# Fourth attention: score product split into three fp32r products with rounded and low parts

## The reference

```python
h = group_norm(x, gn_w, gn_b)
q = nin(h, Wq, bq).reshape(B, C, H * W)        # C = 128, H * W = 1024
k = nin(h, Wk, bk).reshape(B, C, H * W)
v = nin(h, Wv, bv).reshape(B, C, H * W)
w = jnp.einsum('bcn,bcm->bnm', q, k) * C ** (-0.5)
w = jax.nn.softmax(w, axis=-1)
h_out = jnp.einsum('bnm,bcm->bcn', w, v).reshape(B, C, H, W)
h_out = nin(h_out, Wp, bp)
out = (x + h_out) / math.sqrt(2.0)
```

## Time and profile before

| what | value |
| --- | --- |
| three runs | 537.21, 538.37, 539.49 us |
| median | 538.37 us |
| profiled execution, first to last instruction (span) | 533.3 us |
| profiled execution, whole time | not given |
| PE busy in the span | 474.2 us (89%) |
| POOL busy in the span | 277.2 us (52%) |
| granted PE clock, mean | 0.974 |

### The profile page before, as it was taken

How to read it: one execution, slowest core, us unless ns; L and a number is a source line. 1 busy time by engine, 2 the same in 40 slices (tenths; PEclk the granted TensorE clock), 3 DMA queues, 4 the chain that set the end, 5 groups by cost and what they waited for, 6 DMA issues and landing times.

```text
span 533.3 us, 7633 instructions
## 1 busy us (share of the span) xinstructions
PE 474.2 (89%) x2772; PEld 318.4 (60%) x2772; DVE 320.2 (60%) x567; ACT 288.1 (54%) x514; POOL 277.2 (52%) x292
## 2 busy tenths in 40 slices
PE   7997888698768799899988999998989899998997
PEld 3443534336234368567776847775955668693776
DVE  5767775664727667775586665478477446534322
ACT  5464645664746565256566246575635466623653
POOL 0000477777777777777777777777777500000000
PEclk9699999998989889999999999999999999998999
DMA  6000211122131111113112111112111100100001
GB/s 233 0 1 1 75 50 54 51 77 73 52 98 54 50 55 50 55 50 96 55 54 90 55 50 55 49 56 93 52 54 51 44 1 1 40 1 1 1 1 39
DMA packets 12708, 26.94 MB, mean 51 GB/s; under 512 B 4992, under 2 KB 5888, under 8 KB 12672
## 3 DMA queue, kind: packets, MB, share of 16 engines
q0 software_dynamic: 9216, 18.89, 11.9%
q1 hardware_dynamic: 3168, 7.05, 3.7%
q10 hardware_dynamic: 288, 0.52, 0.3%
HBM read 21.99 MB, written 4.46 MB: 50 GB/s over the span
## 4 chain that ended last, share of the span: by engine, by line
POOL 52%; PE 23%; issue 17%; DVE 4%; ACT 3%; DMA 1%; DVEq 1%; POOLq 0%; ACTq 0%
POOL got L337 52%; PE pd L685 5%; PE pq L673 2%; PE pq L412 2%; PE pc L443 1%; PE pc L663 1%; PE pa L663 1%; PE pa L381 1%; DVE neg_max L1774 1%; PE pa L611 1%; PE pc L611 1%; PE pc L381 1%; DMA wts<-weights_dram 1%; PE pa L481 1%; PE pd L611 1%
## 5 line engine op out<-in xcount | busy, mean ns | idle before, releaser
L337 POOL DMA_INDIRECT got<-cell_table,rows_all x288 | 277.0, 962 | 145.4 <-issue 87.5
L1774 DVE TENSOR_REDUCE neg_max<-pa 128x1 f32<-128x1024 f32 x48 | 58.7, 1223 | 31.5 <-PE pa L381 30.7
L1868 DVE TENSOR_TENSOR weighed<-got,pd 128x1152 f32<-128x1152 f32 x32 | 43.2, 1349 | 37.6 <-DMA got<-cell_table,rows_all 19.5
L685 PEld LDWEIGHTS pd<-v3T,probsT 128*128 128x128 f32 x512 | 60.4, 192 | 7.6 <-ACT probsT L1225 5.2
L685 PE MATMUL pd<-v3T,probsT 128*128 128x128 f32 x512 | 63.0, 276 | 1.8 <-ACT probsT L1225 1.8
L412 PE MATMUL pq<-q_stack,k_stack 128*128 128x512 f32 x120 | 52.3, 484 | 6.6 <-ACT expT L1259 3.6
L1259 ACT ACTIVATE expT<-pq 128x512 f32<-128x512 f32 x64 | 35.7, 595 | 21.2 <-PE pq L412 20.2
L381 PE MATMUL pa<-k_stack,q_stack 96*128 96x512 f32 x96 | 36.3, 461 | 7.6 <-DVE neg_max L1774 7.2
L1225 ACT ACTIVATE probsT<-pq 128x1024 f32<-128x1024 f32 (+1 forms) x32 | 32.2, 1006 | 12.3 <-PE pq L673 9.2
L1367 ACT ACTIVATE expT<-pq 128x512 f32<-128x512 f32 x56 | 31.2, 597 | 13.7 <-PE pq L412 12.7
L412 PEld LDWEIGHTS pq<-q_stack,k_stack 128*128 128x128 f32 x120 | 23.0, 203 | 25.2 <-ACT expT L1259 10.4
(11 more groups left out here) (189 smaller groups left out, 800.2 us busy)
## 6 DMA issues: line engine op xcount, KB each, us to landing
got<-cell_table,rows_all POOLq DMA_INDIRECT x288, 2.4
cell_table<-tabS SPq DMA_DIRECT2D x4, 512.0 KB, 2.9
out_dram<-cells SPq DMA_DIRECT2D x7, 256.0 KB
xall<-x_dram SPq DMA_DIRECT2D x3, 512.0 KB, 6.3
wts<-weights_dram SPq DMA_DIRECT2D x1, 778.5 KB, 4.2
xall<-x_dram ACTq DMA_DIRECT2D x2, 256.0 KB, 4.1
cell_table<-tabS SPq DMA_DIRECT2D x4, 64.0 KB, 1.5
wts<-weights_dram SPq DMA_DIRECT2D x1, 215.5 KB, 3.9
```

The lines of the kernel that those rows point to most:

```text
L337: nc.gpsimd.indirect_dma_start(got[:, t, k, :], None, tables[b % 2], bass.IndirectOffsetOnAxis(ap=rows_all[:, b, at:at + 1], axis=0)).then ...
L685: last = nc.tensor.matmul(d0[:, 0:C], probsT[:, tile(j)], v3T[:, j, :], start=j == 0, stop=j == TILES - 1)
L1774: nc.vector.tensor_reduce(neg_max[:, t:t + 1], pair[:, :], axis=X, op=ALU.max, negate=True)\
L1868: nc.vector.tensor_tensor(weighed[:, :, :].rearrange("p k (c r) -> p (k c) r", r=R), got[:, t, :, :].rearrange("p k (c r) -> p (k c) r", r=R),
```

## The change

Keys and queries of block `l3` are kept as two fp32r tensors each. ACT writes the rounded part (bias added) from PSUM, DVE then computes the low part: PSUM value plus bias minus the rounded part. Each half of a tile's scores becomes three accumulated fp32r products: rounded query with rounded key, rounded query with low key, low query with rounded key. The scale of the queries moves into a scaled copy of the weights, `wq3s`, made once at setup. `offs4` gets storage of its own. The steps in the lists of the engines: ACT gains `l3_q`, DVE gains `l3_k`; in batches 0 and 2 keys come first on both, in batches 1 and 3 the first query half, both key halves, the second query half, as on PE. The semaphores `k3_ready` and `q3_ready` now come from the low parts. PE's order is unchanged.

```diff
--- before.py
+++ after.py
@@ -132,8 +132,10 @@
         gstd = sb("gstd", [P, 1])
         gscale = sb("gscale", [P, 1])
         gbias = sb("gbias", [P, 1])
-        q3 = offs4 = sb("q3_offs4", [P, N])
-        k3 = sb("k3", [P, N])
+        offs4 = sb("offs4", [P, N])
+        q3_high, k3_high = sb("q3_high", [P, N], fp32r), sb("k3_high", [P, N], fp32r)
+        q3_low, k3_low = sb("q3_low", [P, N], fp32r), sb("k3_low", [P, N], fp32r)
+        wq3s = sb("wq3s", [P, C])
         v3T = sb("v3T", [P, TILES, C])
         u3 = sb("u3", [P, C])
         gbv2 = sb("gbv2", [P, 1])
@@ -204,8 +206,8 @@
         x3_base = sem("x3_base")
         mom_ready, g_mm = sem("mom_ready"), sem("g_mm")
         gvar_ready, gstd_ready, h3_ready = sem("gvar_ready"), sem("gstd_ready"), sem("h3_ready")
-        k3_mm, k3_ready = sem("k3_mm"), sem("k3_ready")
-        q3_mm, q3_ready = sem("q3_mm"), sem("q3_ready")
+        k3_mm, k3_rounded, k3_ready = sem("k3_mm"), sem("k3_rounded"), sem("k3_ready")
+        q3_mm, q3_rounded, q3_ready = sem("q3_mm"), sem("q3_rounded"), sem("q3_ready")
         v3_mm, v3_ready = sem("v3_mm"), sem("v3_ready")
         s3_mm, max3_done, exp3_done = sem("s3_mm"), sem("max3_done"), sem("exp3_done")
         inv3_done, pt_mm, pt_copied = sem("inv3_done"), sem("pt_mm"), sem("pt_copied")
@@ -643,7 +645,7 @@
 
             def l3_q(b, h):
                 pe.wait_ge(h3_ready, 2 * b + h + 1)
-                nc.tensor.matmul(pc[:, half(h)], wt("wq3"), h3[:, half(h)], start=True, stop=True).then_inc(q3_mm, 1)
+                nc.tensor.matmul(pc[:, half(h)], wq3s[:, :], h3[:, half(h)], start=True, stop=True).then_inc(q3_mm, 1)
 
             def l3_v(b, h):
                 pe.wait_ge(h3_ready, 2 * b + h + 1)
@@ -660,7 +662,10 @@
                     pe.wait_ge(exp3_done, TILES * b + t - 1)
                 pair = (pa, pc)[t % 2]
                 for h in range(2):
-                    last = nc.tensor.matmul(pair[:, half(h)], q3[:, tile(t)], k3[:, half(h)], start=True, stop=True)
+                    own = pair[:, half(h)]
+                    nc.tensor.matmul(own, q3_high[:, tile(t)], k3_high[:, half(h)], start=True, stop=False)
+                    nc.tensor.matmul(own, q3_high[:, tile(t)], k3_low[:, half(h)], start=False, stop=False)
+                    last = nc.tensor.matmul(own, q3_low[:, tile(t)], k3_high[:, half(h)], start=False, stop=True)
                 last.then_inc(s3_mm, 1)
 
             def l3_turn(b, t):
@@ -1384,7 +1389,13 @@
 
             def l3_k(b, h):
                 act.wait_ge(k3_mm, 2 * b + h + 1)
-                nc.scalar.activation(k3[:, half(h)], pa[:, half(h)], ACT.Identity, bias=wt("bk3")).then_inc(k3_ready, 1)
+                nc.scalar.activation(k3_high[:, half(h)], pa[:, half(h)], ACT.Identity, bias=wt("bk3"))\
+                    .then_inc(k3_rounded, 1)
+
+            def l3_q(b, h):
+                act.wait_ge(q3_mm, 2 * b + h + 1)
+                nc.scalar.activation(q3_high[:, half(h)], pc[:, half(h)], ACT.Identity, bias=bq3s[:, :])\
+                    .then_inc(q3_rounded, 1)
 
             def l3_v(b, h):
                 act.wait_ge(v3_mm, 2 * b + h + 1)
@@ -1563,6 +1574,8 @@
             l1_turn(1, 3)
             l3_k(0, 0)
             l3_k(0, 1)
+            l3_q(0, 0)
+            l3_q(0, 1)
             l1_turn(1, 4)
             l3_exp(0, 0)
             l3_v(0, 0)
@@ -1620,8 +1633,10 @@
             load_table(ACT.Sqrt, 2)
             l3_deviation(1)
             load_table(ACT.Exp, 3)
+            l3_q(1, 0)
             l3_k(1, 0)
             l3_k(1, 1)
+            l3_q(1, 1)
             l3_v(1, 0)
             l3_v(1, 1)
             l3_exp(1, 0)
@@ -1683,6 +1698,8 @@
             l3_k(2, 0)
             l3_v(2, 0)
             l3_k(2, 1)
+            l3_q(2, 0)
+            l3_q(2, 1)
             l3_exp(2, 0)
             l3_v(2, 1)
             l1_turn(3, 4)
@@ -1734,8 +1751,10 @@
             l3_residual(3)
             l3_deviation(3)
             load_table(ACT.Exp, 7)
+            l3_q(3, 0)
             l3_k(3, 0)
             l3_k(3, 1)
+            l3_q(3, 1)
             l3_v(3, 0)
             l3_v(3, 1)
             l3_exp(3, 0)
@@ -1923,6 +1942,7 @@
             def l3_weights():
                 nc.vector.tensor_tensor(gbv2[:, :], wt("bv2"), wt("gamma"), ALU.mult)
                 nc.vector.tensor_scalar(bq3s[:, :], wt("bq3"), float(C) ** -0.5, None, ALU.mult)
+                nc.vector.tensor_scalar(wq3s[:, :], wt("wq3"), float(C) ** -0.5, None, ALU.mult)
                 dve.wait_ge(setup_act, 1)
                 nc.vector.tensor_scalar(bp3s[:, :], c1[:, C:C + 1], wt("bp3"), 2.0 ** -0.5, ALU.add, ALU.mult)\
                     .then_inc(setup_act, 1)
@@ -1960,9 +1980,16 @@
                     .then_inc(h3_ready, 1)
 
             def l3_q(b, h):
-                dve.wait_ge(q3_mm, 2 * b + h + 1)
-                nc.vector.tensor_scalar(q3[:, half(h)], pc[:, half(h)], float(C) ** -0.5, bq3s[:, :], ALU.mult, ALU.add)\
+                dve.wait_ge(q3_rounded, 2 * b + h + 1)
+                nc.vector.scalar_tensor_tensor(q3_low[:, half(h)], pc[:, half(h)], bq3s[:, :],
+                                               q3_high[:, half(h)].bitcast(fp32), ALU.add, ALU.subtract)\
                     .then_inc(q3_ready, 1)
+
+            def l3_k(b, h):
+                dve.wait_ge(k3_rounded, 2 * b + h + 1)
+                nc.vector.scalar_tensor_tensor(k3_low[:, half(h)], pa[:, half(h)], wt("bk3"),
+                                               k3_high[:, half(h)].bitcast(fp32), ALU.add, ALU.subtract)\
+                    .then_inc(k3_ready, 1)
 
             def l3_max(b, t):
                 dve.wait_ge(s3_mm, TILES * b + t + 1)
@@ -2160,6 +2187,8 @@
             l3_norm(0, 1)
             l1_weigh(1, 4)
             l1_add(1, 4)
+            l3_k(0, 0)
+            l3_k(0, 1)
             l3_q(0, 0)
             l3_q(0, 1)
             l1_weigh(1, 5)
@@ -2221,6 +2250,8 @@
             l1_weigh(2, 5)
             l1_add(2, 5)
             l3_q(1, 0)
+            l3_k(1, 0)
+            l3_k(1, 1)
             l3_q(1, 1)
             for n in range(4):
                 l3_max(1, n)
@@ -2276,6 +2307,8 @@
             l3_norm(2, 1)
             l1_weigh(3, 4)
             l1_add(3, 4)
+            l3_k(2, 0)
+            l3_k(2, 1)
             l3_q(2, 0)
             l3_q(2, 1)
             l3_max(2, 0)
@@ -2324,6 +2357,8 @@
             l3_norm(3, 0)
             l3_norm(3, 1)
             l3_q(3, 0)
+            l3_k(3, 0)
+            l3_k(3, 1)
             l3_q(3, 1)
             l3_max(3, 0)
             l3_max(3, 1)
```

## The result

The changed kernel runs in 534.76 us (median of 16 executions, 532.35 to 540.82) and the kernel before, on the same chip, in 537.12 us (16 executions, 534.76 to 539.63). The ratio is 0.9958, with a 95% interval of 0.9938 to 0.9978: 2.3 us faster, or 0.42%. Two of the 16 executions of after (540.80 and 540.82) lie over 1.5% above its fastest and are set apart as slow; the median of the other 14 is 534.44 us. The gain is less than the 0.5% by which the prediction calls two times apart. The forecast was -1.98 us and 536.4 us.

A forecast was written before the change was run, and what follows sets the result against it. POOL's gather queue bounds the kernel until 422.9 us, then PE sets a 109 us tail. Terms -0.30 - 1.80 + 0.12 = -1.98 us from the 538.37 median give 536.4 us (-0.37%), range 534.0 to 539.2.

The forecast's parts named there:

- What bounds the kernel: POOL's saturated gather queue covers PE from 58.4 to 422.9 us; the change pays only in the 109 us tail.
- The price of a product: Score products on PE: fp32r products 0.235 us apart, six a tile 1.41 us for 1.72; 0.30 us saved a tile.
- Which tiles count: Score tiles behind the gathers: one of the third batch, -0.30 us, and six of the last batch's eight, -1.80 us.
- Tile 5: Last batch: its saving is lost in a wait for turned tile 3's copy; at most 0.19 of 0.30 us returns, none taken.
- Tile (2,7): Third batch's score tile behind the last gather, PE full on both sides: counts -0.30 us.
- Roundings and low parts: New ACT (0.69 us) and DVE (0.74 us) work: costs 0.12 us before the last batch's first score, nothing in the third.
- The time around the span: Whole time outside the profiled span of 533.3 us: taken as 5.1 us, to the median of 538.37, and unchanged.
- The clock rival: PE's idle before the last sample turn grows, the clock falls behind it: 1.7 us lost, 538.1 us; chance 0.20.
- Loads: PE's six weight loads a tile show: all nine tiles grow by 0.77 us, 545.4 us; chance 0.05.
- Gathers: 12 low parts within the gather stretch each lengthen one POOL gather by 0.56 us: +6.7 us, 543.1 us; chance 0.05.
- More: Score products at 0.215 us give 2.9 us, 535.5 us; with full warm-up clock 533.8 at best; chance 0.12.
- the clock in the warm-up: Before the last batch: full clock kept there takes up to 1.7 us more off; shares the 0.12 chance of more gain.

The follow-up runs named there:

- e9: Changed kernel plus a fourth product (low query with low key) per half in batches 0 to 2, no unread products: 533.03 us, 0.9931 of before.
- e1: Changed kernel with split products in the last batch alone, the other batches plain fp32 as before: 535.12 us, 0.9960 of before.
- e2: Changed kernel with split products in batches 0 to 2 alone, the last batch fp32 as before: 536.05 us, 0.9979 of before.
- e7: Changed kernel plus a fourth product (low with low) per half in batches 0 to 2 and 14 unread products before the last sample turn: 536.69 us, 1.0013.
- e5: Changed kernel, but each score half one fp32 product of rounded parts, low parts unused; 12 unread products before the last sample turn: 536.14 us, 1.0002 of before.
- e4: Kernel before plus 10 unread products in PE's idle before the last sample turn: 535.62 us, 0.9966 of before.
- e3: Changed kernel plus 14 unread products in PE's idle before the last sample turn: 532.73 us, 0.9919 of before.
- e6: Changed kernel plus a fourth product (low with low) per half in the last batch and 14 unread products before the last sample turn: 536.04 us, 0.9991.
- e11: Changed kernel plus 14 unread products before the last sample turn, and 14 instead of 5 in the last batch's first warm-up: 532.64 us, 0.9922 of before.
- e12: Changed kernel plus 14 unread products before the last sample turn, the same kernel as e3 run again: 532.80 us, 0.9932 of before.

## Why the prediction was right, point by point

**What bounds the kernel.** Right. POOL's row is the same in after, e9 holds 11.3 us of extra products without a loss that shows, and e1 with the last batches of e1 and e2 puts the gain into the last batch. The cover has an end, as e7 shows.

**The price of a product.** Right: 0.23 to 0.24 us from start to start, 1.39 to 1.40 us a tile, where the step took 1.41 from the stacks of the second attention. The gap of 216 ns that the Trainium skill gives for an isolated product, under "Back-to-back issue gap" of "TensorE: Matmul & The Clock Gate", was too short here too; the estimate from it was 1.30 us a tile. This kernel's own rows of the same shape were the better source.

**Which tiles count.** Six of eight, and 1.80 us less 0.12 gave -1.68 for the last batch; measured -1.82. The first score came 4.40 us behind the first query product (4.32 before), the rest of the batch gained 1.90. Tile 5 came out as the step says: 0.33 us saved, 0.23 given back in the wait for the copy (2.02 against 1.79 us), so that about 0.1 of it was kept. Tile (2,7): 1.72 to 1.40, -0.32 for -0.30. Together that is -2.14 us on the path, for the -1.98 forecast, and it does not hang on the median.

**Roundings and low parts.** Right in price (687 and 746 to 747 ns for 0.69 and 0.74 us) and nearly in place: e5 shows 0.14 us on the path for 0.12, but only 0.07 of it before the first score, where the sum has all of it.

**The time around the span.** Wrong: 5.1 us were taken, 1.8 are there. The step set the span of one execution against the median of others and took the difference for a constant. It was for the greater part the luck of that execution, which was 2 us under its kernel's median. This did no harm to the forecast, because the sum was subtracted from the median of the runs; whoever had set the span of after, 536.1, against that of before, 533.3, would have called the change 2.8 us slower.

**The clock rival.** The mechanism was right and its place in the argument was wrong. It was told as something that the change may bring on, by stretching an idle of 2.81 us to some 3.4 to 4.3 (3.84 in the profile of after). Two things were mis-sized. The price: 1.7 us were taken from a stretch of 4.3 us; here the clock was low for 6.8 us, which cost 3.21 us on the path, and in e1 and e2 it cost 1.49 and 4.25. And the other side: the term counts only as a difference, and e1 (a fall in an idle of 2.73 us) and e4 (-1.6 us for the fill) say that the kernel before pays it as well. That it cancels to such a degree was not foreseen: with a fall in the profile of after and none in that of before, the median held by luck as far as this term goes. What the change adds to it is not resolved by the runs: the change is worth 2.3 us without fills, and 1.8 and 2.9 with them. One profile of before could not have shown this; its row of 1.00 was one draw of several.

**The other rivals.** Loads did not show: 188 to 190 ns of load for each of six products, and the products still 0.23 us apart. The rule that the Trainium skill gives under "What overlaps and what doesn't" of "TensorE: Matmul & The Clock Gate", by which loads on the same row groups would not be hidden, is not borne out by this kernel before or after. Gathers were not stretched: 276.7 us for 288 of them in after, 277.0 in before, with 12 more low parts beside them. More was not gained in the last batch either: what passes the forecast (-2.3 against -2.0 us of medians) is within the measurement. The other half of that rival, the clock in the warm-up, was priced right: 1.7 us taken, 1.2 to 1.7 in the profiles, and with one fill it was there in e3 and not in e6. (The forecast of 536.4 stands 1.6 us above the 534.76 measured; 1.25 us of that is the median of before, 538.37 in three executions and 537.12 in sixteen.)

**The checks announced.** Six records 0.23 to 0.24 apart: seen. Period 4.08 for 4.38: 4.12 and 4.06. Last gather at 422 within 1 us: 422.42. Idle of 3.4 to 4.3: 3.84. First score 4.3 + 0.1 behind the first query product: 4.40. Clock after 427 at 1.00: it was not, and the forecast held in spite of it, for the reason just given.

## What to carry to other kernels

First ask behind which queue the work lies, and price only what stands behind its end: here 8 of 32 tiles carried the whole gain of the change. Where two profiles disagree with two medians, find out where each profiled execution stands among its own runs before a row is believed, and look for the clock. An idle of PE of a few microseconds just before PE becomes the chain is worth a few unread products, sized to the idle and no longer: they gave 1.4 to 2.1 us here, nearly as much as the change itself, and put 1.2 us (e5) and 3.0 us (e7) on the path where they outlasted the idle.

## What was not expected of the hardware

The clock did not go by the length of the idle. Around the last turn of samples it fell with an idle of 2.73 us (e1), 3.84 (after) and 4.49 (e2), and stayed at 1.00 with 2.81 (before), 1.69 (e9), 1.52 (e11, e12) and everything shorter. In the warm-up it fell with 2.05 us (e3) and not with 2.04 (e6), and at 461 it fell with gaps of 0.5 us (e12) and not with the same gaps (e11). Nor did it fall at one point of the idle: read from stretches of 1 us, it fell 0.2 and 1.2 us before PE began again in e1 and e2, and 1.2 us behind it in after, with PE busy. How long it stayed down differed too, with PE busy throughout: 3 us behind the last turn in e1, 8 us in after, 9 us in e2. What decides it is open; that falls come and go is seen between kernels that are alike at the place in question. They set executions apart: from the last turn of samples to the first query product the profiles range from 57.92 us (e11, no fall) to 63.83 (e2, two falls).

The landing of a gather varies as well: the last one took 2.39 us (e4) to 3.75 us (after) from its start, with nothing queued behind it. In the profile of after that alone put 1.2 us on the path. Its cause is open.
